# A fused attention and expert layer: the clamped sum in front of a tile's last row maximum, and GpSimd's work held until it is done

## The chip, the cores and the metric

The kernel runs on 1 core of one Trainium2 chip. The metric is the device time of one execution in microseconds (us); lower is better.

## The reference, cut to what matters

Input x is 4096 tokens of 256 features. The first half of the layer is an attention with 16 heads of 16 features and an additive bias that depends on both tokens:

```
q, k, v      = linear(layernorm(x)), split in 16 heads
scores[h]    = q k^T / 4
logits[i,j,:] = li[i,:] + lj[j,:] + rel_b          (3 relations)
bias[h,i,j]  = sum_r softmax(logits[i,j])[r] * logical_bias[h,r]
scores[h]   += gate[i,h] * bias[h,i,j]
out          = softmax(scores) v, then a linear layer, added to x
```

The second half is a layer norm and a mixture of 8 experts, of which each token takes its best 2; its result is added too.

The softmax over three relations needs two differences of logits per pair of tokens, one exponential each, their sum plus one, and the reciprocal of that.

## The kernel before, in words

There are three stages: `project_inputs`, `attend` and `experts`. The change touches only `attend`.

`attend` goes over 32 query chunks `c` of 128 queries, and in each over 32 key tiles `jt` of 128 keys. Chunks 0 to 23 run in a hardware loop that holds 8 chunks; the others are written out. Each engine has its own instruction queue in an order fixed by hand, and engines wait for each other only by counting semaphores (`s["..."]`).

For one key tile (L879 on, L686 on, L762 on):

- TensorE writes the scores of tile `jt + 1` into `b_sc` (`pe_scores`: first `pe_relation`, L801, for each half, then `pe_products`, L813). Each half has one buffer, so a half is overwritten only when the exponential that read it is done. Then come the first row-maximum pair (`pe_pair`, L832), the value product of tile `jt` (`pe_pv`, L855, which needs both exponentials of `jt`), and the second row-maximum pair.
- ScalarE takes the exponentials of both halves of tile `jt` (L690, 128x1024 each). After an even tile it takes the exponential of two clamped sums (`act_r_exp`, L668). After an odd tile it takes a logarithm and an exponential of the sum that GpSimd made of them (`act_r_inv`, L675 and L677); that is the reciprocal.
- VectorE reduces the two row-maximum pairs, four maxima of 128x512 from a ring of three banks, `b_mx` (`dve_pair`, L716), for the coming query chunks, and then makes one clamped sum (`dve_d`, L708, "the clamp": add a constant per query, take the minimum with 43). After tile 23 it also finishes the maxima of a chunk (`dve_m`, L722 and L726). After the first pair of tile 31 it copies the accumulator (L733).
- GpSimd goes by turns of two tiles, turn `t` being tiles `2t` and `2t + 1`. In a turn it adds the two exponentials (`pool_sum`, L613, "the addition"), in turns 13 and 14 it makes half of `b_cm` for the next chunk (`pool_c`, L604), and then it splits the reciprocal into two f16 parts (`pool_parts`: the cast, L623, and the subtraction, L625).
- SP copies these parts into `b_rst` (L526), from where TensorE reads them as weights for the bias. A unit of 512 keys is four tiles; during one unit SP copies the next, and GpSimd makes the one after that.

The work on the relations runs ahead: turn `t` handles the key group `g = t + 4` (`R_AHEAD`), and the clamp made at tile `jt` has the number `8 + jt + 3` counted from the start of the chunk (`D_AHEAD` is 3). So what turn `t` adds has been clamped some tiles before.

Two buffers hold the clamped sums and two the exponentials, so a clamp also waits until the exponential of two groups before has been taken.

Of the kernel before, what the change touches and what calls it, by code (L numbers as in the profile page):

```python
# [29 lines left out]
NT = S // P  # L30
# [7 lines left out]
UNITS = S // JU  # L38
# [15 lines left out]
PAIRN = PAIRS * MXU  # L54
# [5 lines left out]
R_AHEAD, D_AHEAD = 4, 3  # L60
CLAMP_SLOT, ACC_SLOT = 1, 0
# [5 lines left out]
def step_ring(jt, slot):  # L67

    return START + 4 * jt + 2 * slot + (1 if jt > OUT_AT else 0)


def step_bank(jt, slot):

    return step_ring(jt, slot) % MX_RING
# [23 lines left out]
def identity_into(nc, pool, t, zeroed, made):  # L98

    nc.gpsimd.memset(t, 0.0).then_inc(zeroed, 1)  # L100
    pool.wait_ge(zeroed, 1)
    nc.gpsimd.affine_select(out=t, in_=t, compare_op=ALU.not_equal, fill=1.0, base=0,
                            pattern=[[-1, P]], channel_multiplier=1).then_inc(made, 1)
# [341 lines left out]
def attend(nc, kst, vp, dj_dram, q_dram, c_dram, const_dram, m_dram, att_dram):  # L445

    with ExitStack() as ctx:
# [3 lines left out]
        def sem(name):  # L451
            return ctx.enter_context(nc.semaphore("b_" + name))
# [32 lines left out]
        s = {n: sem(n) for n in names}  # L485
# [111 lines left out]
        def pool_c(pool, x, par, nth, half):  # L597

            if half == 0:
                pool.wait_ge(s[f"cval_in{par}"], 96 * nth)  # L600
                pool.wait_ge(s["m_in"], 32 * (x + 1))
                if not (isinstance(x, int) and x < 2):
                    pool.wait_ge(s["scores_ready"], STEPS * (x - 1))
            nc.gpsimd.tensor_tensor(cm[:, par, half],  # L604
                                    cval[:, par, :, half:H:2].unsqueeze(3).broadcast_to([P, NB, PAIRS, BI]),
                                    eye[:, :].unsqueeze(1).unsqueeze(1).broadcast_to([P, NB, PAIRS, BI]),
                                    ALU.mult).then_inc(s["c_made"], 1)

        def pool_sum(pool, x, g):

            n = 16 * x + g
            pool.wait_ge(s["e_ready"], n + 1)
            nc.gpsimd.tensor_tensor(ex[:, g % 2, 0], ex[:, g % 2, 0], ex[:, g % 2, 1], ALU.add).then_inc(s["sum_ready"], 1)  # L613

        def pool_parts(pool, x, g):

            u, n = g // 2, 16 * x + g
            pool.wait_ge(s["r_ready"], n + 1)
            if not (isinstance(x, int) and x == 0 and u < 2):
                pool.wait_ge(s[f"r_in{u % 2}"], 96 * (UNITS // 2 * x + u // 2))  # L620
            pool.sem_inc(s["pool_waited"], 1)
            slot = 2 * (u % 2) + g % 2
            nc.gpsimd.tensor_copy(rhi[:, slot], ex[:, g % 2, 0]).then_inc(s["hi_ready"], 1)  # L623
            pool.wait_ge(s["hi_ready"], n + 1)
            nc.gpsimd.tensor_tensor(rlo[:, slot], ex[:, g % 2, 0], rhi[:, slot], ALU.subtract).then_inc(s["lo_ready"], 1)  # L625

        @block.gpsimd
        def _(pool):
            identity_into(nc, pool, ident[:, :], s["zeroed"], s["ident_made"])
            nc.gpsimd.memset(cval[:, :, :, :], 0.0).then_inc(s["cval_zeroed"], 1)  # L630
            nc.gpsimd.memset(att[:, :, :], 0.0).then_inc(s["att_zeroed"], 1)
            nc.gpsimd.memset(eye[:, :], 0.0).then_inc(s["eye_made"], 1)
            first_rows = [32 * m + part for m in range(4) for part in range(PARTS) if part < PARTS - 1 or m % 2 == 0]
            for n, row in enumerate(first_rows):
                pool.wait_ge(s["eye_made"], n + 1)
                nc.gpsimd.affine_select(out=eye[:, :], in_=eye[:, :], compare_op=ALU.not_equal, fill=1.0,
                                        base=-row, pattern=[[-PARTS, BI]], channel_multiplier=1).then_inc(s["eye_made"], 1)
            pool.wait_ge(s["eye_made"], len(first_rows) + 1)
            for g in range(R_AHEAD):
                pool_sum(pool, 0, g)  # L640
                pool_parts(pool, 0, g)
            for half in range(2):
                pool_c(pool, 0, 0, 1, half)

            def chunk(c, par, nth, last, slot4):
                for turn in range(2 * UNITS):
                    g = turn + R_AHEAD
                    if g < 2 * UNITS:
                        pool_sum(pool, c, g)
                    elif not last:  # L650
                        pool_sum(pool, c + 1, g - 2 * UNITS)
                    if turn in C_MAPS and not last:
                        pool_c(pool, c + 1, 1 - par, nth + par, C_MAPS.index(turn))
                    if g < 2 * UNITS:
                        pool_parts(pool, c, g)
                    elif not last:
                        pool_parts(pool, c + 1, g - 2 * UNITS)

            in_chunks(pool, chunk)


# [39 lines left out]
        def dve_d(dve, x, par, nth, g, n):  # L701

            u, side = g // 2, g % 2
            if g == 0 and n == 0:
                dve.wait_ge(s[f"const_in{par}"], 80 * nth)
            if n == 0 and not (isinstance(x, int) and x == 0 and g < 2):
                dve.wait_ge(s["e_ready"], 16 * x + g - 1)
            nc.vector.tensor_scalar(dl[:, side, n], dj[:, u, n], const[:, par, side, n:n + 1], EXP_MAX, ALU.add,  # L708
                                    ALU.min).then_inc(s["d_ready"], 1)

        def dve_pair(dve, x, n, bank):

            for ab in range(2):
                dve.wait_ge(s["mx_ready"], 2 * PAIRN * x + 2 * n + ab + 1)
                head, part = 2 * (n // MXU) + ab, n % MXU
                nc.vector.tensor_reduce(mxp[:, head, part:part + 1], mx[:, (bank + ab) % MX_RING, :], AX.X,  # L716
                                        ALU.max).then_inc(s["mx_used"], 1)
# [11 lines left out]
        def dve_acc(dve, c):  # L729

            dve.wait_ge(s["pv_done"], NT * c + NT)
            dve.wait_ge(s["o_turned"], c + 1)
            nc.vector.tensor_copy(oT[:, :, :], acc[:, :, :]).then_inc(s["acc_read"], 1)  # L733
# [11 lines left out]
        @block.vector  # L745
        def _(dve):
            nc.vector.memset(oT[:, :, :], 1.0).then_inc(s["acc_read"], 1)
            nc.vector.memset(rst[:, :, :, :], 1.0).then_inc(s["ones_made"], 1)
            dve.wait_ge(s["dj_in0"], 32)
            for n in range(PAIRN):  # L750
                if n % 2 == 0 and n < 2 * R_AHEAD:
                    for k in range(2):
                        dve_d(dve, 0, 0, 1, n // 2, k)
                dve_pair(dve, 0, n, 2 * n)
            dve_m(dve, 0, 0, 1)
            for n in range(AHEAD):
                dve_pair(dve, 1, n, 2 * PAIRN + 2 * n)
            dve.wait_ge(s["dj_in1"], 16 * (UNITS - 2))
            for n in range(D_AHEAD):
                dve_d(dve, 0, 0, 1, R_AHEAD + n // 2, n % 2)  # L760

            def chunk(c, par, nth, last, slot4):  # L762
                more = not last and not (isinstance(c, int) and c + 2 >= NT)
                for jt in range(NT):
                    for slot in range(2):
                        n = 2 * jt + slot + AHEAD
                        if n < PAIRN and not last:
                            dve_pair(dve, c + 1, n, step_bank(jt, slot))
                        elif n >= PAIRN and more:
                            dve_pair(dve, c + 2, n - PAIRN, step_bank(jt, slot))  # L770
                        if slot == CLAMP_SLOT:
                            g, k = R_AHEAD + (jt + D_AHEAD) // 2, (jt + D_AHEAD) % 2
                            if g < 2 * UNITS:
                                dve_d(dve, c, par, nth, g, k)
                            elif not last:
                                dve_d(dve, c + 1, 1 - par, nth + par, g - 2 * UNITS, k)
                        if n + 1 == PAIRN and not last:
                            dve_m(dve, c + 1, 1 - par, nth + par)
                        if jt == NT - 1 and slot == ACC_SLOT:
                            dve_acc(dve, c)  # L780
                    if jt == OUT_AT:
                        dve_out(dve, c)

            in_chunks(dve, chunk)
            dve_out(dve, NT)

# [682 lines left out]
```

## Time and profile before

| | before |
|---|---|
| time, median of 3 runs | 4546.25 us (4544.65 to 4565.15) |
| profiled execution: time | 4540.25 us |
| profiled execution: span | 4538.5 us |
| granted TensorE clock, mean of the span | 0.944 |
| VectorE (DVE) busy | 3815.9 us, 84% |
| TensorE (PE) busy | 3592.7 us, 79% |
| ScalarE (ACT) busy | 3321.6 us, 73% |
| GpSimd (POOL) busy | 2042.4 us, 45% |

The attention loop takes the stretch from about 343 to 3680 us; before it are the projections and the row maxima of the first chunks, and behind it are the experts. The shares are means over all three stages. Times in the rows are us, "mean ns" is of one instruction.

### The profile page before, as it was taken

What the parts mean: (1) busy time and instruction counts of PE and PEld (TensorE: products, weight loads), DVE (VectorE), ACT (ScalarE), POOL (GpSimd) and SP (SyncE); (2) the same over time, 40 slices, a digit from 0 to 9 for tenths busy, and PEclk for the clock granted to TensorE, in tenths of its full rate; (3) what the DMA queues carried; (4) which work ended last, traced back from release to release, by engine and by line L of the source; (5) the groups of instructions that cost most, each with busy time, mean ns of one, the idle gap of its engine ahead of it and who ended that gap; (6) DMA issues with size and microseconds to landing.
All of it is one profiled execution on the core that took longest, in us unless ns stands there. A gap on an engine that the chain in (4) does not pass through costs nothing. (4 is left out here: it accounts for less than half of the span.)

```text
span 4538.5 us, 243862 instructions
## 1 busy us (share of the span) xinstructions
PE 3592.7 (79%) x106896; PEld 2680.9 (59%) x106896; DVE 3815.9 (84%) x6310; ACT 3321.6 (73%) x3946; POOL 2042.4 (45%) x1816
## 2 busy tenths in 40 slices
PE   7548888888888888888888888888888866399991
PEld 4306666666566666656666666666666655277771
DVE  4299999999899999999999999999999814277773
ACT  2008888988898898988898989999999961144440
POOL 0014445554454555544454555555555531533335
PEclk8659999999999999999999999999999996699996
DMA  5312222222222222222222222222222244344433
GB/s 105 73 38 68 67 68 68 71 70 66 65 70 67 67 69 70 66 67 68 66 70 67 71 69 68 68 70 66 75 64 70 67 120 140 121 151 147 154 127 120
DMA packets 368338, 371.66 MB, mean 82 GB/s; under 512 B 108416, under 2 KB 342272, under 8 KB 363296
## 3 DMA queue, kind: packets, MB, share of 16 engines
q1 hardware_dynamic: 358080, 338.08, 27.3%
q8 instruction: 857, 14.04, 1.3%
q0 software_dynamic: 6144, 16.79, 1.2%
q14 instruction: 217, 1.78, 0.1%
q10 hardware_dynamic: 3040, 0.98, 0.1%
HBM read 99.58 MB, written 46.40 MB: 32 GB/s over the span
## 5 line engine op out<-in xcount | busy, mean ns | idle before, releaser
L716 DVE TENSOR_REDUCE b_mxp<-b_mx 128x1 f32<-128x512 f32 x4096 | 2572.8, 679 | 126.5 <-PE b_mx L832 102.2
L690 ACT ACTIVATE b_pr<-b_sc 128x1024 f32<-128x1024 f32 x2048 | 1982.0, 1020 | 418.5 <-PE b_sc L813 399.8
L855 PE MATMUL b_acc<-b_pr,vp 128*32 128x128 f32 x32768 | 1141.4, 276 | 29.5 <-issue 27.1
L832 PE MATMUL b_mx<-kst,b_qt 64*128 64x512 f16 x4096 | 818.9, 393 | 413.1 <-DVE b_mxp L716 397.1
L855 PEld LDWEIGHTS b_acc<-b_pr,vp 128*32 128x32 f32 x32768 | 845.6, 110 | 287.4 <-issue 281.7
L613 POOL TENSOR_TENSOR b_ex<-b_ex 128x512 f32<-128x512 f32 x512 | 679.3, 1327 | 604.8 <-ACT b_ex L668 599.4
L801 PE MATMUL b_sc<-b_cm,b_rst 64*128 64x64 f16 x32768 | 765.8, 191 | 169.4 <-ACT b_pr L690 90.4
L801 PEld LDWEIGHTS b_sc<-b_cm,b_rst 64*128 64x128 f16 x32768 | 657.6, 95 | 338.1 <-ACT b_pr L690 147.0
L708 DVE TENSOR_SCALAR b_dl<-b_dj,b_const 128x512 f32<-128x512 f32 x1024 | 774.1, 758 | 67.9 <-ACT b_ex L668 39.2
L623 POOL CAST b_rhi<-b_ex 128x512 f16<-128x512 f32 x512 | 320.5, 626 | 1064.6 <-ACT b_ex L677 761.0
L813 PE MATMUL b_sc<-b_qt,kst 64*128 64x64 f16 x32768 | 686.4, 191 | 45.7 <-issue 42.0
L625 POOL TENSOR_TENSOR b_rlo<-b_ex,b_rhi 128x512 f16<-128x512 f32 x512 | 633.9, 1238 | 41.0
L813 PEld LDWEIGHTS b_sc<-b_qt,kst 64*128 64x128 f16 x32768 | 571.7, 95 | 67.2 <-issue 64.2
L832 PEld LDWEIGHTS b_mx<-kst,b_qt 64*128 64x128 f16 x4096 | 201.0, 94 | 691.1 <-DVE b_mxp L716 663.8
L668 ACT ACTIVATE b_ex<-b_dl 128x1024 f32<-128x1024 f32 x512 | 541.7, 1058 | 37.4 <-DVE b_dl L708 37.4
L677 ACT ACTIVATE b_ex<-b_ex 128x512 f32<-128x512 f32 x512 | 322.7, 630 | 16.1
L675 ACT ACTIVATE b_ex<-b_ex 128x512 f32<-128x512 f32 x512 | 323.4, 632 | 8.6 <-POOL b_ex L613 8.6
L1314 ACT ACTIVATE c_h<-c_ps,c_b1b 128x512 f32<-128x512 f32 x184 | 126.6, 688 | 276.7 <-PE c_ps L1347 229.7
L1347 PE MATMUL c_ps<-c_xT,c_w1p 128*128 128x512 f16 x1104 | 258.4, 385 | 9.9 <-DVE c_xT L1184 9.8
L1358 PE MATMUL c_ps<-c_w2p,c_a 128*128 128x256 f16 x2208 | 255.4, 273 | 0.0
L1358 PEld LDWEIGHTS c_ps<-c_w2p,c_a 128*128 128x128 f16 x2208 | 216.0, 98 | 36.0
L1071 POOL TENSOR_TENSOR c_w1p<-c_w1r,c_w1p 128x2048 f16<-128x2048 f32 x22 | 90.1, 4094 | 280.2 <-ACT c_w1p L1284 280.2
(144 smaller groups left out, 1753.0 us busy)
## 6 DMA issues: line engine op xcount, KB each, us to landing
b_rst<-b_rhi SPq DMA_DIRECT2D x1024, 128.0 KB
b_rst<-b_rlo SPq DMA_DIRECT2D x512, 128.0 KB
c_w1r<-in_L_ffn_W_dram SPq DMA_DIRECT2D x23, 1024.0 KB, 4.9
c_w2r<-in_L_ffn_W_dram SPq DMA_DIRECT2D x23, 1024.0 KB, 4.9
expert_tokens<-c_zeros SPq DMA_DIRECT2D x23, 512.0 KB, 6.6
c_xb<-expert_tokens SPq DMA_DIRECT2D x23, 512.0 KB
expert_results<-c_y SPq DMA_DIRECT2D x23, 512.0 KB, 2.8
b_qt<-q_parts SPq DMA_DIRECT2D x64, 128.0 KB
```

The lines of the kernel that those rows point to most:

```text
L613: nc.gpsimd.tensor_tensor(ex[:, g % 2, 0], ex[:, g % 2, 0], ex[:, g % 2, 1], ALU.add).then_inc(s["sum_ready"], 1)
L625: nc.gpsimd.tensor_tensor(rlo[:, slot], ex[:, g % 2, 0], rhi[:, slot], ALU.subtract).then_inc(s["lo_ready"], 1)
L668: nc.scalar.activation(ex[:, k].rearrange("p n j -> p (n j)"), dl[:, k].rearrange("p n j -> p (n j)"), ACT.Exp).then_inc(s["e_ready"], 1)
L675: nc.scalar.activation(ex[:, k, 0], ex[:, k, 0], ACT.Ln, bias=1.0).then_inc(s["ln_ready"], 1)
L690: nc.scalar.activation(pr[:, jt % 2, half, :], sc[:, half].rearrange("p a b -> p (a b)"), ACT.Exp).then_inc(s["p_ready"], 1)
L708: nc.vector.tensor_scalar(dl[:, side, n], dj[:, u, n], const[:, par, side, n:n + 1], EXP_MAX, ALU.add, ALU.min).then_inc(s["d_ready"], 1)
L716: nc.vector.tensor_reduce(mxp[:, head, part:part + 1], mx[:, (bank + ab) % MX_RING, :], AX.X, ALU.max).then_inc(s["mx_used"], 1)
L801: ins = pe.matmul(out, rst[rows, u % 2, b, j0:j0 + P], cm[rows, par, half, b], start=(b == 0), stop=False, skip_group_check=True)
L813: ins = pe.matmul(sc[:, ab, side, pair * IS:pair * IS + IS], kst[rows, pair, jt * P:jt * P + P], qt[rows, slot4, pair, side * IS:side * IS ...
L832: pe.matmul(mx[:, (bank + ab) % MX_RING, :], qt[rows, slot4, pair, :], kst[rows, pair, j0:j0 + 512], start=True, stop=True).then_inc(s["mx ...
L855: ins = pe.matmul(acc[32 * (h % 4):32 * (h % 4) + 32, h // 4, :], vp[:, jt, VW * h:VW * h + 32], pr[:, jt % 2, h % 2].rearrange("p (a h i) ...
L1358: ins = pe.matmul(ps[:, 4 + d % 2, 0:D], hT[:, b % 2, hp, f, t * P:t * P + P], w2p[:, b % 2, wp, f, :], start=(f == 0 and hp == 0 and wp = ...
```

## The change

The clamp of a tile stood behind the tile's four row maxima on VectorE; it now stands behind the third and in front of the fourth. GpSimd has two new waits per turn: it goes on to the addition of turn `t` only when VectorE has finished the clamp of tile `2t`, and to the cast only when it has finished the clamp of tile `2t + 1`. `pool_sum` also gets a count on `pool_waited` between that wait and the old one.

```diff
+        def after_clamp(pool, c, jt, last):
+
+            count = 32 * c + 2 * R_AHEAD + D_AHEAD + jt + 1
+            pool.wait_ge(s["d_ready"], min(count, 32 * NT) if last else count)
+
         def pool_sum(pool, x, g):
 
             n = 16 * x + g
+            pool.sem_inc(s["pool_waited"], 1)
             pool.wait_ge(s["e_ready"], n + 1)
...
                 for turn in range(2 * UNITS):
                     g = turn + R_AHEAD
+                    after_clamp(pool, c, 2 * turn, last)
                     if g < 2 * UNITS:
                         pool_sum(pool, c, g)
                     elif not last:
                         pool_sum(pool, c + 1, g - 2 * UNITS)
                     if turn in C_MAPS and not last:
                         pool_c(pool, c + 1, 1 - par, nth + par, C_MAPS.index(turn))
+                    after_clamp(pool, c, 2 * turn + 1, last)
                     if g < 2 * UNITS:
                         pool_parts(pool, c, g)
...
-        def dve_pair(dve, x, n, bank):
-
-            for ab in range(2):
+        def dve_pair(dve, x, n, bank, halves=range(2)):
+
+            for ab in halves:
...
-                        if n < PAIRN and not last:
-                            dve_pair(dve, c + 1, n, step_bank(jt, slot))
-                        elif n >= PAIRN and more:
-                            dve_pair(dve, c + 2, n - PAIRN, step_bank(jt, slot))
-                        if slot == CLAMP_SLOT:
-                            g, k = R_AHEAD + (jt + D_AHEAD) // 2, (jt + D_AHEAD) % 2
-                            if g < 2 * UNITS:
-                                dve_d(dve, c, par, nth, g, k)
-                            elif not last:
-                                dve_d(dve, c + 1, 1 - par, nth + par, g - 2 * UNITS, k)
+                        for ab in range(2):
+                            if slot == CLAMP_SLOT and ab == 1:
+                                g, k = R_AHEAD + (jt + D_AHEAD) // 2, (jt + D_AHEAD) % 2
+                                if g < 2 * UNITS:
+                                    dve_d(dve, c, par, nth, g, k)
+                                elif not last:
+                                    dve_d(dve, c + 1, 1 - par, nth + par, g - 2 * UNITS, k)
+                            if n < PAIRN and not last:
+                                dve_pair(dve, c + 1, n, step_bank(jt, slot), (ab,))
+                            elif n >= PAIRN and more:
+                                dve_pair(dve, c + 2, n - PAIRN, step_bank(jt, slot), (ab,))
```

## Rows read from the trace of the kernel before

**Rows 1.** Busy us (x instructions) by stretch: PE, PEld, DVE, ACT, POOL, clock, DMA.

```profile
343.00:350.00 7.00, 5.58 (x134) 4.05 (x130) 2.74 (x6) 5.97 (x7) 1.26 (x1) 0.50 0.43 115
343.00:3593.00 3250.00, 2719.67 (x98646) 2042.46 (x98640) 3124.68 (x5077) 2924.70 (x3449) 1641.20 (x1537) 1.00 0.26 68
3616.00:3677.00 61.00, 47.08 (x1920) 38.05 (x1911) 20.23 (x22) 58.62 (x70) 30.12 (x31) 1.00 0.27 71
```

**Rows 2.** Waits, 343 to 3593: total us, times, longest us.

```profile
PEld b_mx L832 <- DVE b_mxp L716: 528.4, 933, 1.8
```

**Rows 3.** Instruction groups, 343 to 3593: busy us, mean ns of one, idle before.

```profile
L716 DVE TENSOR_REDUCE b_mxp<-b_mx 128x1 f32<-128x512 f32 x3936 | 2469.8, 679 | 118.8 <-PE b_mx L832 102.2
L708 DVE TENSOR_SCALAR b_dl<-b_dj,b_const 128x512 f32<-128x512 f32 x987 | 740.5, 750 | 0.0
```

**Rows 4.** Timeline of VectorE, 2011 to 2028: start us, duration us, instruction.

```profile
2011.69 1.44 DVE L708 TENSOR_SCALAR b_dl<-b_dj,b_const 128x512 f32<-128x512 f32 x1
2013.05 0.27 DVE L722 TENSOR_REDUCE b_mrow<-b_mxp 128x16 f32<-128x128 f32 x1
...
2022.53 0.71 DVE L708 TENSOR_SCALAR b_dl<-b_dj,b_const 128x512 f32<-128x512 f32 x1
...
2027.71 0.69 DVE L716 TENSOR_REDUCE b_mxp<-b_mx 128x1 f32<-128x512 f32 x1 [0.38 <-PE b_mx L832]
```

**Rows 5.** Timeline of GpSimd, 2011 to 2028.

```profile
2011.57 1.28 POOL L613 TENSOR_TENSOR b_ex<-b_ex 128x512 f32<-128x512 f32 x1 [1.18 <-ACT b_ex L668]
...
2018.66 1.27 POOL L613 TENSOR_TENSOR b_ex<-b_ex 128x512 f32<-128x512 f32 x1 [1.93 <-ACT b_ex L668]
2019.89 1.22 POOL L604 TENSOR_TENSOR b_cm<-b_cval,b_eye 128x512 f16<-128x512 f16 x1
2022.35 0.61 POOL L623 CAST b_rhi<-b_ex 128x512 f16<-128x512 f32 x1 [1.24 <-ACT b_ex L677]
```

**Rows 6.** Timeline of ScalarE, 2015 to 2025.

```profile
2017.53 1.06 ACT L668 ACTIVATE b_ex<-b_dl 128x1024 f32<-128x1024 f32 x1
...
2020.86 0.63 ACT L675 ACTIVATE b_ex<-b_ex 128x512 f32<-128x512 f32 x1
2021.53 0.63 ACT L677 ACTIVATE b_ex<-b_ex 128x512 f32<-128x512 f32 x1
2022.80 1.94 ACT L690 ACTIVATE b_pr<-b_sc 128x1024 f32<-128x1024 f32 x2 [0.64 <-PE b_sc L813]
```

**Rows 7.** Timeline of all engines before the loop, 228 to 231.

```profile
228.93 1.26 POOL L613 TENSOR_TENSOR b_ex<-b_ex 128x512 f32<-128x512 f32 x1 [34.05 <-ACT b_ex L668]
...
230.22 0.63 ACT L675 ACTIVATE b_ex<-b_ex 128x512 f32<-128x512 f32 x1 [1.45 <-POOL b_ex L613]
```

**Rows 8.** Timeline of ScalarE in the last query chunk, 3630 to 3680.

```profile
3630.28 0.63 ACT L675 ACTIVATE b_ex<-b_ex 128x512 f32<-128x512 f32 x1
...
3636.19 0.63 ACT L675 ACTIVATE b_ex<-b_ex 128x512 f32<-128x512 f32 x1
...
3637.39 1.92 ACT L690 ACTIVATE b_pr<-b_sc 128x1024 f32<-128x1024 f32 x2
...
3679.09 0.63 ACT L675 ACTIVATE b_ex<-b_ex 128x512 f32<-128x512 f32 x1
```

**Rows 9.** Timeline of TensorE's matmuls, 2022 to 2028.

```profile
2022.69 0.39 PE L832 MATMUL b_mx<-kst,b_qt 64*128 64x512 f16 x2
2023.01 1.08 PE L855 MATMUL b_acc<-b_pr,vp 128*32 128x128 f32 x32
2024.03 0.39 PE L832 MATMUL b_mx<-kst,b_qt 64*128 64x512 f16 x2
...
2025.51 0.38 PE L832 MATMUL b_mx<-kst,b_qt 64*128 64x512 f16 x2
...
2027.29 0.39 PE L832 MATMUL b_mx<-kst,b_qt 64*128 64x512 f16 x2
```

**Rows 10.** Timeline of TensorE's matmuls at the loop's start, 343 to 350.

```profile
346.54 0.62 PE L832 MATMUL b_mx<-kst,b_qt 64*128 64x512 f16 x2
...
348.96 0.61 PE L832 MATMUL b_mx<-kst,b_qt 64*128 64x512 f16 x2
```

## The prediction, made before the changed kernel was built or run

> **What bounds the kernel now.** I read the busy time by stretch first [rows 1]. The attention stage from 343 to 3593 us is 3250 us long; VectorE is busy for 3125 of them (96%), ScalarE for 2925 (90%), TensorE for 2720 and GpSimd for 1641. In the 61 us of the last query chunk, where no row maxima are left to compute, ScalarE takes over (58.6 us busy) and VectorE falls to 20. So VectorE paces the stage and ScalarE stands right behind it. The waits say the same from the other side: TensorE's weight load for the row-maximum product waited 933 times, 528 us in all, until VectorE had freed a bank [rows 2].
>
> I count in turns: one GpSimd turn spans two key tiles, 2t and 2t+1. The row-maximum work that can tie VectorE to TensorE runs in chunks 0 to 29 (16 turns each) and the first 12 turns of chunk 30, so 492 turns. 3250 us / 492 = 6.61 us per turn now.
>
> In a turn VectorE makes 8 row maxima, 0.68 us each, and 2 clamped sums of mean 0.75 us [rows 3]. A free clamped sum takes 0.47 us, one that meets GpSimd's addition 1.44 us: the addition holds from 2011.57 to 2012.85, the clamp begins at 2011.69 and ends at 2013.13 [rows 4, 5]. That is what the change can win: 987 clamps x (0.75 - 0.47) = 276 us of VectorE's time.
>
> The Trainium skill ("SBUF — State Buffer", section "SBUF: two separate sides") has a rule for this pair of engines: an instruction of the one that uses the shared port pair holds it until it ends, and the other is fully blocked. The 1.44 us clamp agrees. Taken alone, the rule speaks for the change and would have the whole 276 us come back; that result is the third rival below, priced there from rows.
>
> **Where the new wait lands.** This is the step on which everything hangs, so I place the tiles in the trace. The small reduction at 2013.05 is the one that follows key tile 23, so the clamp at 2011.69 is tile 23's, and three clamps on, at 2022.53, is tile 26's [rows 4]. On GpSimd, the product that writes b_cm first comes behind the addition of turn 13; it stands at 2019.89, so the addition at 2018.66 is turn 13's, which belongs to tile 26 [rows 5]. After the change that addition may not start until the clamp of tile 26 is done. Now it starts 3.87 us ahead of that clamp. The ordering is not close: VectorE works on tile 26's maxima long after ScalarE has finished tile 26.
>
> Moving the clamp in front of the last of the tile's four maxima brings it forward by one maximum, 0.61 us. The addition would still be released only at 2022.53 - 0.61 + 0.47 = 2022.39, plus 0.19 us for the signal (an exponential that ends at 2022.16 releases the cast at 2022.35, with the same wait and count in front of it) [rows 5, 6]: 3.92 us later than now. What covers it is small: the addition ends at 2019.93 and ScalarE's logarithm that reads it starts at 2020.86 [rows 5, 6], 0.93 us of cover. And ScalarE runs its queue in order: behind that logarithm wait the second exponential of the same sum and then the two softmax exponentials of tile 28.
>
> **The loop that the wait closes.** Nothing now makes the addition depend on the same tile's clamp; the clamps run three ahead. With the wait there is a ring through all four engines, once per turn. From the end of the clamp of tile 2t:
> - signal to GpSimd 0.19, the addition 1.28, signal to ScalarE 0.03 (an addition that ends at 230.19 releases the logarithm at 230.22) [rows 5, 7]: 1.50;
> - ScalarE: from the logarithm's start to the start of the softmax exponentials of tile 2t+2, 1.20 [rows 8], and those two exponentials, 1.94 [rows 6]: 3.14;
> - TensorE: the scores tensor has one buffer per half, so the scores of tile 2t+3 are finished only after both exponentials of 2t+2, and in the written order they, the first row-maximum pair and the value product all come ahead of the second pair. Exponentials end at 2024.74, pair starts at 2025.51: 0.77. Pair to value product 0.32, value product to the second pair 1.02 [rows 9]: 2.11;
> - from that pair's start to the start of its maximum on an idle VectorE 0.42 (2027.29 to 2027.71) [rows 4, 9], one maximum 0.61, the clamp, alone now, 0.47: 1.50.
>
> Sum 1.50 + 3.14 + 2.11 + 1.50 = 8.25 us per turn. VectorE's own work in it is 8 x 0.61 + 2 x 0.47 = 5.8 us, so it waits; ScalarE's is about the 5.91 us of a turn that it alone paces (3630.28 to 3636.19) [rows 8], so it idles some 2.3 us between the softmax of the odd tile and the late logarithm. Both end below the ring, which therefore is the bound: the collisions on the port are gone and nothing is won by it.
>
> Real turns are a bit longer than clean ones: in the last chunk 8 turns from 3630.28 to 3679.09 take 6.10 us each against 5.91 [rows 8]. Part of such hiccups will fall into engines that now idle; of 0.19 I take 0.15. So 8.40 us per turn, 1.79 more than now, x 492 = 881 us.
>
> **The other parts of the edit.** The cast's wait (for the clamp of tile 2t+1) is in no ring. In the new turn that clamp ends about 2.9 us after tile 2t's does, with the addition (1.28) and, in two turns of sixteen, the b_cm product (1.22) before it on GpSimd, and what the cast feeds, the copies by SP's queue into b_rst, is for a key unit whose use begins four tiles later. I cost it at nothing; the cover is that unit, about two turns. Behind the waiting cast stand the subtraction and the next addition, which waits longer for its own clamp anyway. No DMA is moved; SP's copies only go out later, inside that cover. The additional count on pool_waited rides in the 0.19. The later last maximum (0.47 us) can delay a bank of the ring of three, but the first pair of the next tile needs only the bank of the maximum ahead of the clamp: nothing. In the last chunk, and the last 4 turns of chunk 30, there are no maxima; both clamps of a turn are done before its addition can start, so the waits are met at once and that stretch stays.
>
> Bounds of the ring: what I can't see is whether each piece is as long in the ring as where I read it. With TensorE's and VectorE's pieces read too long by queued work, 8.1 us; with every hiccup on the ring and the 1.22 us product partly on it, 8.9. That is 733 to 1127 us.
>
> The profiled execution took 4540.25 us (span 4538.5), 6 us under the median of 4546.25. 4540 + 881 = 5421, and with those 6 us and the rounding of the ring I say 5430 us. The likeliest case's own range is 5280 to 5680.
>
> **Rivals.**
> - *TensorE's clock drops.* In the ring TensorE idles about 1.9 us in one piece per turn, behind the second pair of the odd tile. The granted clock is 1.00 over the present loop (2.4 GHz) [rows 1]. At 1.2 GHz, as from 343 to 350 us [rows 1], pair to pair takes 2.42 instead of 1.34 us [rows 9, 10]; the 0.77 stretched in that ratio gives 0.62 more, the feeding pair 0.22 more (0.61 against 0.39): the ring is 8.40 + 1.92 = 10.3 us, + 1820 us, some 6370. Against it: at that clock TensorE has almost no idle time in a turn, and after 343 us it was in just such a stretch that it rose. The Trainium skill ("TensorE: Matmul & The Clock Gate", section "Part 1: The HAM clock gate (the 'warmup' mystery)") says that an idle stretch throttles the clock and sustained work releases it; by that this rival would oscillate between both levels and land near 5900.
> - *VectorE keeps its lag.* If the clamp stays as late against ScalarE as now, each turn pays 3.92 - 0.93 = 2.99 us: 9.60 us per turn, +1471, 6020 us. Against it: VectorE has 2.4 us to spare per turn and catches up.
> - *The wait is met in time and the port is what counts.* The other side. If VectorE, relieved, ran so far ahead that the clamp of tile 2t ended before ScalarE's exponential of the same turn, the addition would lose nothing, and the turn would fall by two times 0.28 us, to 6.05; ScalarE's pace of 6.10 [rows 8] is then the bound: (6.61 - 6.10) x 492 = 251 us, so 4295 us. It decides at the point where the lag of 3.9 us is zero; but the maximum in front of that clamp needs a product that TensorE issues behind tile 2t's value product, which needs tile 2t's softmax, and the exponential starts when the softmax ends. The clamp can't come first, since TensorE's 2.11 us and the 1.50 behind it are more than the exponential's 1.06 [rows 6]; this rival needs my reading of the order to be wrong.
> - *A shorter ring.* If TensorE's modelled records overstate its stretch (2.11 becomes 1.3), the ring is 7.5 to 7.6 us: + 460 or so, about 5000 us.
> - *Nothing happens* (the count in the wait is one that is always met): 4546 us. The count is 32c + 12 + tile, and clamps are numbered so that this includes the tile's own.
>
> **Chances.** Forecast 0.76, clock 0.07, lag 0.06, shorter ring 0.05, faster 0.04, nothing 0.02. The range reaches into the shorter ring and the oscillating clock, 5180 to 5760. A difference of under 0.5% (23 us) can't be told from none; slower by more 0.94, within it 0.02, faster 0.04.
>
> **What would show it.** The additions start 8.2 to 8.6 us apart, each about 0.2 us behind the end of a clamp, and the logarithm starts at the addition's end: ScalarE's largest wait becomes GpSimd's addition, about 2 us x 492 = 1000 us in all, where now it is not in the list. Nearly all clamps of the loop take 0.47 us (mean under 0.55). VectorE's busy share of the stretch falls to about 70% and its waits for TensorE's row-maximum product grow by hundreds of us. The third stage keeps its length. I am wrong if the additions keep a spacing under 7.5 us, if ScalarE doesn't wait for GpSimd, or if the granted clock is under 0.95 in the loop.

## The result, and the profile after

| | before | after |
|---|---|---|
| time, median of 4 runs | 4551.01 us (4544.65 to 4565.15) | 5823.51 us (5818.44 to 5830.7) |
| ratio, 95% interval | | 1.2787 (1.2764 to 1.281) |
| profiled execution: time | 4540.25 us | 5819.15 us |
| span | 4538.5 us | 5817.4 us |
| granted TensorE clock, mean | 0.944 | 0.859 |

The change makes the kernel 27.9% slower. I forecast slower, 5430 us with a range of 5180 to 5760; the measured time lies above the range. One execution of the kernel before (5645 us) and one of e12 below (4532 us) ran at a lower granted clock throughout; the ratios leave them out.

Busy time by stretch in the changed kernel, with the columns of [rows 1]. The first row is the loop, the second is the last chunk, the third is the expert stage.

```profile
343.00:4880.00 4537.00, 3222.13 (x98892) 2309.31 (x98896) 2945.73 (x5080) 2948.11 (x3459) 1562.37 (x1541) 0.87 0.19 49
4890.00:4951.00 61.00, 47.89 (x1915) 38.01 (x1906) 19.68 (x24) 58.84 (x71) 30.47 (x31) 1.00 0.27 71
4978.00:5817.00 839.00, 599.90 (x4208) 474.04 (x4208) 470.12 (x825) 253.95 (x312) 331.51 (x189) 0.84 0.42 141
```

All of the loss is in the loop. The last chunk runs as before [rows 1], and in the expert stage, 839 us here, the engines are busy for practically the same time as in the last 838 us of the kernel before (TensorE 600 and 598 us). In the loop VectorE is busy for 65% (96% before) and ScalarE for 65% (90%). No engine bounds it any more. And TensorE's clock is at 0.87 where it was 1.00.

The waits of the loop, 343 to 4880 us, with the columns of [rows 2]:

```profile
POOL b_ex L619 <- DVE b_dl L716: 2165.9, 483, 23.7
DVE b_mxp L724 <- PE b_mx L841: 1562.1, 852, 6.9
...
ACT b_ex L683 <- POOL b_ex L619: 1492.4, 492, 3.8
PE b_sc L810 <- ACT b_pr L698: 1279.6, 1144, 5.0
```

Read as a circle they name the ring: GpSimd waits for the clamp, ScalarE for GpSimd (492 times, the number of turns that the prediction counts), TensorE for ScalarE, VectorE for TensorE. Before, the long wait was TensorE's for VectorE [rows 2], a bounding engine's sign.

Two of the costly groups of the whole changed kernel, with the columns of [rows 3]:

```profile
L724 DVE TENSOR_REDUCE b_mxp<-b_mx 128x1 f32<-128x512 f32 x4096 | 2663.7, 685 | 1586.8 <-PE b_mx L841 1562.1
L716 DVE TENSOR_SCALAR b_dl<-b_dj,b_const 128x512 f32<-128x512 f32 x1024 | 504.5, 494 | 68.0 <-ACT b_ex L676 39.8
```

The clamps fell from a mean of 0.75 us [rows 3] to 0.49 (0.48 in the loop): the collisions are gone. The idle time in front of the maxima, 1587 us, is far more than what that saved.

One turn of the changed kernel, 3006.9 to 3016.7 us, put together from the timelines of the four engines. First GpSimd and ScalarE:

```profile
3006.93 1.27 POOL L619 TENSOR_TENSOR b_ex<-b_ex 128x512 f32<-128x512 f32 x1 [5.12 <-DVE b_dl L716]
...
3016.74 1.27 POOL L619 TENSOR_TENSOR b_ex<-b_ex 128x512 f32<-128x512 f32 x1 [4.63 <-DVE b_dl L716]
```

```profile
3008.24 0.63 ACT L683 ACTIVATE b_ex<-b_ex 128x512 f32<-128x512 f32 x1 [3.21 <-POOL b_ex L619]
...
3009.43 1.92 ACT L698 ACTIVATE b_pr<-b_sc 128x1024 f32<-128x1024 f32 x2
3011.24 1.06 ACT L676 ACTIVATE b_ex<-b_dl 128x1024 f32<-128x1024 f32 x1
```

Then TensorE, and VectorE's maximum and clamp:

```profile
3010.50 0.41 PE L810 MATMUL b_sc<-b_cm,b_rst 64*128 64x64 f16 x16 [2.16 <-ACT b_pr L698]
3011.41 0.41 PE L810 MATMUL b_sc<-b_cm,b_rst 64*128 64x64 f16 x16 [0.51 <-ACT b_pr L698]
3011.65 0.90 PE L822 MATMUL b_sc<-b_qt,kst 64*128 64x64 f16 x32
3012.36 0.62 PE L841 MATMUL b_mx<-kst,b_qt 64*128 64x512 f16 x2
3012.91 1.94 PE L864 MATMUL b_acc<-b_pr,vp 128*32 128x128 f32 x32
3014.77 0.61 PE L841 MATMUL b_mx<-kst,b_qt 64*128 64x512 f16 x2
```

```profile
3015.41 0.69 DVE L724 TENSOR_REDUCE b_mxp<-b_mx 128x1 f32<-128x512 f32 x1 [1.12 <-PE b_mx L841]
3016.02 0.48 DVE L716 TENSOR_SCALAR b_dl<-b_dj,b_const 128x512 f32<-128x512 f32 x1
```

The steps follow each other without a pause. From start to start: the addition to the logarithm 1.31, to the softmax exponentials 1.19, their length 1.92, to the first pair 1.01, to the value product 0.55, to the second pair 1.86, to the clamp 1.25, its length 0.48, the signal 0.24. Sum 9.81 us, the whole turn. The ring is there as predicted; but TensorE's steps are long. The gap of 2.16 us ends at 3010.50, the first products behind it still take 0.41 for sixteen, and then the pair takes 0.62 instead of 0.39 and the value product 1.94 instead of 1.08 [rows 9]. Such durations are those at 1.2 GHz [rows 10], and the granted clock of these stretches, the third number from the end of each row, says the same:

```profile
3005.00:3011.80 6.80, 3.94 (x153) 2.74 (x146) 5.07 (x9) 3.56 (x6) 2.72 (x3) 1.00 0.25 61
3011.90:3015.20 3.30, 3.30 (x66) 2.08 (x60) 1.29 (x2) 2.34 (x3) 0.22 (x1) 0.50 0.40 104
3015.30:3016.70 1.40, 1.40 (x76) 1.17 (x76) 1.29 (x3) 0.00 (x0) 0.00 (x0) 1.00 0.10 29
```

The clock falls behind the gap, when TensorE has begun to work again, and is back before the turn ends.

Between 1000 and 3040 us the trace has 219 steps from one addition to the next: 63 of 8.3 us, 75 of 9.8, most of the rest from 9.2 to 9.7. The mean is 9.29. The 155 steps longer than 8.7 us all hold a stretch with the clock at 1.2 GHz, and the 64 others hold none.

### The profile page after: what moved, and what is told of

It is laid out like the page before. It is cut to its first block and busy times, and to the rows that moved or that the text cites. A ratio compares the mean times of both kernels' runs of the same rounds, so it can differ in the third digit from the quotient of the medians.

```text
span 5817.4 us, 245654 instructions
## 1 busy us (share of the span) xinstructions
PE 4086.5 (70%) x106896; PEld 2939.9 (51%) x106896; DVE 3632.4 (62%) x6310; ACT 3338.7 (57%) x3946; POOL 1959.7 (34%) x1816
## 3 DMA queue, kind: packets, MB, share of 16 engines
q10 hardware_dynamic: 3040, 0.98, 0.1%
## 5 line engine op out<-in xcount | busy, mean ns | idle before, releaser
L724 DVE TENSOR_REDUCE b_mxp<-b_mx 128x1 f32<-128x512 f32 x4096 | 2663.7, 685 | 1586.8 <-PE b_mx L841 1562.1
L810 PE MATMUL b_sc<-b_cm,b_rst 64*128 64x64 f16 x32768 | 855.0, 200 | 1302.4 <-ACT b_pr L698 1294.8
L810 PEld LDWEIGHTS b_sc<-b_cm,b_rst 64*128 64x128 f16 x32768 | 697.9, 101 | 1635.3 <-ACT b_pr L698 1522.2
L864 PE MATMUL b_acc<-b_pr,vp 128*32 128x128 f32 x32768 | 1390.0, 322 | 1.4 <-ACT b_pr L698 1.0
L864 PEld LDWEIGHTS b_acc<-b_pr,vp 128*32 128x32 f32 x32768 | 1026.0, 128 | 319.7 <-issue 287.6
L841 PE MATMUL b_mx<-kst,b_qt 64*128 64x512 f16 x4096 | 922.0, 446 | 132.2 <-DVE b_mxp L724 118.7
L822 PEld LDWEIGHTS b_sc<-b_qt,kst 64*128 64x128 f16 x32768 | 620.8, 100 | 5.0 <-issue 4.6
L631 POOL TENSOR_TENSOR b_rlo<-b_ex,b_rhi 128x512 f16<-128x512 f32 x512 | 592.5, 1157 | 40.9
L716 DVE TENSOR_SCALAR b_dl<-b_dj,b_const 128x512 f32<-128x512 f32 x1024 | 504.5, 494 | 68.0 <-ACT b_ex L676 39.8
L1202 DVE TENSOR_TENSOR c_a<-c_h,c_a 128x512 f16<-128x512 f32 x184 | 210.3, 1143 | 6.3
```

Source lines behind the costliest of these rows:

```text
L810: ins = pe.matmul(out, rst[rows, u % 2, b, j0:j0 + P], cm[rows, par, half, b], start=(b == 0), stop=False, skip_group_check=True)
L822: ins = pe.matmul(sc[:, ab, side, pair * IS:pair * IS + IS], kst[rows, pair, jt * P:jt * P + P], qt[rows, slot4, pair, side * IS:side * IS ...
L841: pe.matmul(mx[:, (bank + ab) % MX_RING, :], qt[rows, slot4, pair, :], kst[rows, pair, j0:j0 + 512], start=True, stop=True).then_inc(s["mx ...
L864: ins = pe.matmul(acc[32 * (h % 4):32 * (h % 4) + 32, h // 4, :], vp[:, jt, VW * h:VW * h + 32], pr[:, jt % 2, h % 2].rearrange("p (a h i) ...
```

## Experiments

Each kernel was timed beside the kernel before on the same chip. "Ratio" is against it, with its 95% interval.

### e1 and e5: keep TensorE at work in the gap

The question was how much of the loss is the ring and how much the clock. Both kernels are the changed one with more work for TensorE: extra products into a bank that the next pair overwrites, in the place where TensorE idles.

The edit, cut to what matters:

```diff
+ # e5, behind every odd tile; e1: tiles 3 to 29 but 23, and FILL = 6
+ pe.wait_ge(s["mx_used"], unit - 1 if jt == OUT_AT else unit - 2)
+ for _ in range(FILL):            # FILL = 8
+     pe.matmul(mx[:, bank, :], qt[0:64, slot4, 0, :], kst[0:64, 0, 0:512], start=True, stop=True)
```

> The changed kernel with added TensorE work: after the second row-maximum pair of each odd tile from 3 to 29, six extra products are issued into the bank that the next tile's first pair will overwrite anyway (about 1.3 us at 2.4 GHz), in the gap in which TensorE idles about 2 us. Nothing of the ring through the four engines changes. Theory (ring of 8.3 us per turn, stretched to 9.2 to 9.8 by the clock that falls in the gap): the granted clock of the loop goes back above 0.95, nearly all turns take 8.3 us, and the time falls to 5430 (5350 to 5550) although TensorE does more. Rival (the ring itself is 9.2 us, the clock is only a sign of the idling): the time stays within 1% of 5824. Rival (VectorE's lag sets it): no less than 5824, rather more.

e1 measured 5640.85 us, ratio 1.2415 (1.2356 to 1.2473). Of 229 turns 133 took 8.3 us, but 65 still took 9.8: only part of the effect, and the forecast was missed. Its trace still shows where the clock falls, behind a gap that was not filled:

```profile
3004.70 0.39 PE L842 MATMUL b_mx<-kst,b_qt 64*128 64x512 f16 x2
3006.60 0.41 PE L811 MATMUL b_sc<-b_cm,b_rst 64*128 64x64 f16 x16 [1.51 <-ACT b_pr L699]
3007.51 0.55 PE L811 MATMUL b_sc<-b_cm,b_rst 64*128 64x64 f16 x16 [0.51 <-ACT b_pr L699]
3007.88 1.04 PE L823 MATMUL b_sc<-b_qt,kst 64*128 64x64 f16 x32
```

> As e1, but eight extra products instead of six, and behind every odd tile (e1 left out tiles 1, 23 and 31, and its full turns still left 0.5 us of the long gap). Clock theory: e1 had 8.3 us turns and 9.8 us turns, the latter where the clock was at 1.2 GHz; with the gap closed the 9.8 us turns nearly vanish, granted clock of the loop above 0.97, mean turn 8.3 to 8.5, time 5400 to 5500. Rival (the long turns come from something else, which the extra products only shift): 5641 as e1 within 1%, or more because of the added work.

e5 measured 5375.69 us (5374.25 to 5375.86), ratio 1.1833 (1.1809 to 1.1856). 235 of 244 turns took 8.3 us. Its loop by stretch, columns of [rows 1], and one turn on TensorE:

```profile
343.00:4430.00 4087.00, 3664.11 (x102612) 2325.55 (x102612) 2959.70 (x5078) 2941.91 (x3451) 1558.54 (x1537) 1.00 0.21 54
```

```profile
3007.08 1.90 PE L868 MATMUL b_mx<-kst,b_qt 64*128 64x512 f16 x8
3008.98 0.41 PE L811 MATMUL b_sc<-b_cm,b_rst 64*128 64x64 f16 x16
3009.89 0.41 PE L811 MATMUL b_sc<-b_cm,b_rst 64*128 64x64 f16 x16 [0.51 <-ACT b_pr L699]
3010.13 0.64 PE L823 MATMUL b_sc<-b_qt,kst 64*128 64x64 f16 x32
3010.61 0.38 PE L842 MATMUL b_mx<-kst,b_qt 64*128 64x512 f16 x2
3010.92 1.08 PE L876 MATMUL b_acc<-b_pr,vp 128*32 128x128 f32 x32
3011.93 0.39 PE L842 MATMUL b_mx<-kst,b_qt 64*128 64x512 f16 x2
```

The eight extra products (1.90 us) fill the gap, the clock stays at 1.00 (2.4 GHz), and the kernel is 448 us faster than the changed one while TensorE does more. The turn now is 8.27 us (additions at 3005.41 and 3013.68), against the 8.25 that was added up beforehand. So of the 1273 us lost, 448 are the clock, and 5376 - 4551 = 825 are the ring at full clock. By the ratios, each taken beside the kernel before on one chip, it is 434 and 834: about a third and two thirds.

### e6 and e7: one wait at a time

```diff
  # e6: the addition's wait alone
  after_clamp(pool, c, 2 * turn, last)
...
- after_clamp(pool, c, 2 * turn + 1, last)
  # e7: the cast's wait alone
- after_clamp(pool, c, 2 * turn, last)
...
  after_clamp(pool, c, 2 * turn + 1, last)
```

> The changed kernel without the cast's wait; the addition still waits for the clamp of tile 2t. Ring theory: the cast is in no ring, so the time is that of the changed kernel, 5824 within 1%. Rival (both waits share the cost): between 4424 and 5824, some 5100.

5828.13 us, ratio 1.2821 (1.2791 to 1.285): all of the loss is the addition's wait.

> The changed kernel without the addition's wait; the cast still waits for the clamp of tile 2t+1. Ring theory: no ring, the time of the moved clamp alone, 4424 within 1%. Rival (both waits share the cost): some 5100.

4564.46 us, ratio 1.0053 (1.0035 to 1.007). A miss: 140 us above the moved clamp alone (e3 below). The cast's wait does close a ring, a longer one that spans two turns. Timelines of GpSimd and ScalarE in this kernel:

```profile
2006.83 0.61 POOL L629 CAST b_rhi<-b_ex 128x512 f16<-128x512 f32 x1 [3.60 <-DVE b_dl L715]
2007.52 1.16 POOL L631 TENSOR_TENSOR b_rlo<-b_ex,b_rhi 128x512 f16<-128x512 f32 x1
2008.64 1.27 POOL L619 TENSOR_TENSOR b_ex<-b_ex 128x512 f32<-128x512 f32 x1
```

```profile
2009.94 0.63 ACT L682 ACTIVATE b_ex<-b_ex 128x512 f32<-128x512 f32 x1 [0.66 <-POOL b_ex L619]
...
2011.14 1.92 ACT L697 ACTIVATE b_pr<-b_sc 128x1024 f32<-128x1024 f32 x2
```

The clamp of the odd tile (ends 2006.58) releases the cast; the subtraction and the next turn's addition are queued behind it with no pause, and ScalarE's logarithm waits for that addition. Clamp to logarithm 3.36, to the softmax 1.20, two tiles of softmax with the exponential between 1.82 + 1.09 + 1.94, TensorE 2.11, to the end of the clamp 1.50: 13.0 us for two turns, 6.5 per turn. The measured mean is 6.70, against 6.42 in e3. The TensorE and clamp pieces of this sum are the prediction's, but the sum shows as a floor: between 1000 and 3000 us none of 296 pairs of turns takes less than 12.9 us, where in e3 202 of 310 do. Clamps that meet GpSimd's instructions (mean 0.56 us, against 0.50 in e3) are not in it. In the changed kernel this ring hides behind the longer ring.

### e4 and e8: make the ring longer and shorter

e4 is the changed kernel with the clamp back behind the fourth maximum; e8 has it in front of the third.

```diff
- if slot == CLAMP_SLOT and ab == 1:
+ if slot == CLAMP_SLOT and ab == 0:      # e8
```

> Only the two waits of GpSimd; the clamp stays behind the fourth maximum. Ring theory: the ring gains one maximum, 0.61 us, so 8.3 + 0.6 = 8.9 us at full clock, and with the same stretches at 1.2 GHz some 9.8 to 10.0 on average: 5824 + 492 x 0.61 = 6120 us (6050 to 6250). Rival (VectorE is not in the path, its order is free): 5824 within 1%.

6337.43 us, ratio 1.3958 (1.3894 to 1.4022). The direction is right and the size isn't: 514 us more than the changed kernel, not 300, and above the range. Nearly every turn takes 10.2 us (185 of 198), and the granted clock of the loop is 0.83: with the longer gap the clock falls in every turn, 194 times in 194 turns between 1000 and 3000 us, against 152 times in 215 in the changed kernel. Per turn e4 costs 1.04 us more, of which the maximum is 0.61; what is left goes with the clock.

> The changed kernel with the clamp in front of the third of the tile's four maxima instead of the fourth; both waits stay. The ring then doesn't pass the value product (1.02), the step from the first pair to it (0.32) and takes one maximum more on VectorE behind the first pair (0.61): 8.3 - 1.34 + 0.61 = 7.5 to 7.6 us at full clock, 0.75 less than the changed kernel. With the clock held, (7.55 - 6.6) x 492 + 4545 = 5010 us; with it falling as often as now some 5450. So 5000 to 5450. Rival (the order on VectorE doesn't matter, the wait costs its 3 us against ScalarE anyway): 5800 within 2%. Rival (only VectorE's maximum ahead of the clamp counts, as between the changed kernel and the waits-only one): 5824 - 0.61 x 492 = 5520.

5025.03 us, ratio 1.1062 (1.104 to 1.1085). 216 of 268 turns take 7.5 us, where 7.5 to 7.6 had been added up; the clock of the loop is 0.95. One turn, from the addition at 2003.50 to that at 2011.03, put together from TensorE, VectorE and GpSimd:

```profile
2008.69 0.38 PE L841 MATMUL b_mx<-kst,b_qt 64*128 64x512 f16 x2
2009.00 1.08 PE L864 MATMUL b_acc<-b_pr,vp 128*32 128x128 f32 x32
2009.11 1.29 DVE L724 TENSOR_REDUCE b_mxp<-b_mx 128x1 f32<-128x512 f32 x2 [1.75 <-PE b_mx L841]
2010.31 0.47 DVE L716 TENSOR_SCALAR b_dl<-b_dj,b_const 128x512 f32<-128x512 f32 x1
2011.03 1.27 POOL L619 TENSOR_TENSOR b_ex<-b_ex 128x512 f32<-128x512 f32 x1 [2.83 <-DVE b_dl L716]
```

The clamp comes 1.62 us behind the start of the first pair, and the value product runs beside the two maxima in between: the ring no longer passes it. The rival by which only one maximum counts would give 8.27 - 0.61 = 7.66 us at full clock; 7.53 was measured. Its price of 5520 us was 500 us off mostly because it left the clock as low as in the changed kernel. Against e5, whose clock stays full, e8 gains 351 us, 0.71 per turn.

### e2: ask for one clamp less

```diff
- count = 32 * c + 2 * R_AHEAD + D_AHEAD + jt + 1
+ count = 32 * c + 2 * R_AHEAD + D_AHEAD + jt
```

> The changed kernel with both new waits asking for one clamp less: the addition of turn t waits for the clamp of tile 2t-1, the cast for that of tile 2t. Theory of the ring: the addition then depends on a clamp whose product was issued before ScalarE's exponential of the same turn, the ring spans two turns with 1.50+1.20+1.94+0.95+1.94+2.11+1.50 = 11.1 us, 5.6 per turn, below ScalarE's 5.9 to 6.1, so it doesn't bind; clamps stay at 0.48 us. ScalarE bounds: 6.1 to 6.3 us per turn, 4290 to 4400 us, faster than before. Rival (each wait on VectorE costs its signal and the order, whatever clamp it asks for): slower than before by some per cent, 4650 or more. Rival (port gain is nothing on the path): within 1% of before.

4419.37 us, ratio 0.9728 (0.9682 to 0.9774), 20 us above the expected 4290 to 4400 but on the right side: faster than before. Its loop by stretch, and its clamps between 400 and 3400 us:

```profile
343.00:3460.00 3117.00, 2743.41 (x98222) 2031.14 (x98222) 2897.36 (x5055) 2896.48 (x3435) 1552.73 (x1531) 1.00 0.27 71
```

```profile
L716 DVE TENSOR_SCALAR b_dl<-b_dj,b_const 128x512 f32<-128x512 f32 x943 | 450.2, 477 | 0.0
```

VectorE and ScalarE are both busy for 93%. Between this and the 5824 us of the changed kernel there is one count in each of the two waits.

### e3, e9 to e12: what the moved clamp is worth

e3 and e12 are the same kernel: the clamp in front of the fourth maximum, no new waits. e9 has it in front of the third, no waits. e10 has it behind the fourth, as before, and both waits as in e2. e11 has it in front of the third and the waits of e2.

> Only the clamp is moved in front of the last row maximum; GpSimd has no new waits (the extra count on pool_waited stays). Ring theory: no ring, so about before: 4550, between 4450 and 4620, since the clamp only meets GpSimd's instructions at other moments. Rival (the move itself costs, by a late bank of the ring of three): 4700 or more. The mean clamp says which: near 0.75 us as before, or shorter if the new place misses the additions.

> The clamp in front of the third maximum, GpSimd without the new waits. The moved clamp alone gave 4424 us, with a mean clamp of 0.50 us instead of 0.75. If the gain of the move is only that clamps miss GpSimd's instructions, it depends on where the clamp then falls: with another 0.6 us earlier it should still mostly miss them, 4400 to 4450, mean clamp under 0.6. Rival (the gain came from the order on VectorE as such, an earlier freed bank): a further gain, 4380 or less, or its loss, 4500 or more, whatever the clamps take.

> The clamp stays behind the fourth maximum as before; GpSimd has both waits, asking for one clamp less than the changed kernel. Ring over two turns: 11.1 + 0.6 = 11.7 us, 5.9 per turn, at ScalarE's own pace, so it may bind a little. All clamps 0.48 us by the waits. If the collisions on the port were the loss of the kernel before, this gets about the same 4420 (4400 to 4480) without the move. Rival (the move's gain is from its place): 4540 within 1%.

> The clamp in front of the third maximum and both waits asking for one clamp less. No ring of one turn; clamps 0.48 us. ScalarE and VectorE both near 5.9 us per turn: 4400 to 4430, the same as e2 within 0.5%. Rival (some 0.6 us of lateness of GpSimd still costs): 20 to 60 us less than e2's 4419.

> The moved clamp alone once more, beside the other candidates on the same chip: 4424 within 0.5%; e2 and it were not told apart.

| | time, us | ratio | mean single clamp, 1000 to 3000 us |
|---|---|---|---|
| before | | 1 | 0.72 |
| e3 | 4423.63 | 0.9737 (0.9691 to 0.9783) | 0.50 |
| e12 | 4454.68 | 0.9775 (0.9754 to 0.9796) | 0.51 |
| e9 | 4441.14 | 0.9748 (0.9726 to 0.9769) | 0.64 |
| e10 | 4462.76 | 0.9795 (0.9775 to 0.9816) | 0.48 |
| e11 | 4451.44 | 0.9766 (0.9739 to 0.9793) | 0.63 |

e3 and e9 to e12 gain 2.0 to 2.6%. e3 was expected between 4450 and 4620 and came out below, a miss: the move alone is worth as much as the move with the harmless waits of e2. e12, its repetition, was expected within 0.5% of 4424 and came out at 4455, in a round in which the kernel before was 15 us slower too; the ratios of e3 and e12 agree.

Without any wait the clamps of e3 and e12 mostly miss the additions. Two forecasts on the clamps missed: in e9 they were expected under 0.6 us and take 0.64, and in e11, expected at 0.48 by its waits, they take 0.63, with a time above the 4400 to 4430 expected. Why the waits of e11 don't keep them apart is open. So the gain does not follow the clamp: e9, with clamps of 0.64 us, is no slower than e12 with 0.51. Between 1000 and 3000 us 235 of its 617 clamps take over 0.55 us, about the share of the kernel before (203 of 604). e10, with no collisions in the old order, gains 2.0%, so the place in the order is not needed for most of the gain; how much of it each of the two causes has in e3 stays open.

The mean turns of these kernels are 6.4 to 6.5 us (6.6 before). ScalarE's own pace, 5.91 us per turn when clean and 6.10 over the last chunk [rows 8], lies under all of these means; what fills the difference was not tested. e2, e3, e9 and e11 can't be told apart; the simplest that beats both kernels is e3, the moved clamp alone.

## Why the prediction was wrong

- **What bounds, and where the wait lands.** Right. In the turn shown the addition starts at 3016.74, 4.4 us after the exponentials that it adds are ready (3012.30), and e6 shows that this wait is the whole loss. The signal from VectorE takes 0.24 us, not the 0.19 of the sum.
- **The ring at full clock, 8.25 us.** Right: 8.27 in e5, 7.5 in e8 where the same pieces less the value product gave 7.5 to 7.6, and 63 turns of 8.3 in the changed kernel itself. It is also what ends the rival in which VectorE keeps its lag (9.60 us per turn).
- **TensorE's piece of the ring.** This is the step that failed. "Pair to value product 0.32, value product to the second pair 1.02", with the 0.77 ahead of them, took 2.11 us from rows at 2.4 GHz. In the turn shown they take 0.55, 1.86 and 1.01, 3.42 us in all, and the step on to the clamp 1.25 instead of 1.03. The sum had TensorE at 2.4 GHz in every turn. The ring makes TensorE idle for 2.2 us once per turn, in 155 turns of 219 the clock falls, and in the turn shown it is low, at 0.50 from 3011.9 to 3015.2 us, just where TensorE's piece lies on the ring. On average that is 448 us / 492 = 0.91 us per turn. The granted clock of the loop, 0.87, is under the 0.95 that the prediction gave as a sign of being wrong.
- **The rival that named this got 0.07.** I argued that at 1.2 GHz TensorE has almost no idle time and so rises again. It does, before the turn is over; and then comes the next gap. A clock that recovers doesn't exclude one that falls again in most turns. Its pair to pair of 2.42 us was right for a slow turn (3012.36 to 3014.77); its 1.39 for the step ahead of it was too long, since the clock fell within that step, which took 1.01. The oscillating price in that paragraph, near 5900, was 1.3% from the measured 5824 and stood beyond the upper end of the range. It was no sum of its own: it is halfway between 5430 and 6370, and how much of a turn the clock would be low was not worked out, so its closeness is luck.
- **Hiccups, 0.15 us per turn.** Too much, without weight: e5's mean turn is 8.34, 0.07 above its clean one.
- **The cast's wait at nothing.** Wrong by itself (140 us, e7), hidden behind the longer ring here (e6 against the changed kernel: 5 us).
- **The clamps.** Right: 0.49 us mean. ScalarE's wait for the addition was forecast at about 1000 us; it is 1492 in the changed kernel and 1107 at full clock, in e5. VectorE's busy share was forecast at about 70% and is 65%.
- **The faster rival.** Its condition, a wait that is met in time, does not hold here. With one clamp less asked for it does: the clamps take 0.48 us and the kernel runs at 0.973. That is still 4419 us and not the 4295 of the rival, and e9 gains as much with collisions about as frequent as before. That the port is the cause of the gain is not shown.

## What to carry to other kernels

Before adding a wait between two engines, follow the awaited instruction back through its operands and through each queue's order: if the path comes back to the waiting one within a turn, the sum of that path is the new period, however idle all engines look. A wait that asks for one item less can leave that ring. And where the new ring leaves TensorE idle once per turn, cost TensorE's steps behind the gap at 1.2 GHz as well, and let the range hold both.

## What the runs showed of the hardware

- With a gap of 2.2 us in TensorE's work per turn the granted clock of the loop was 0.87, where it had been 1.00. Adding useless products in the gap raised it to 1.00 and made the kernel 7.7% faster (5824 to 5376 us).
- Partial filling gave part of it back: e1, which filled 13 gaps of 16 and those not to the end, got 0.92 and 5641 us. e4, with a maximum more on the ring, got 0.83 and was slow in every turn; e8, with the shorter ring, got 0.95.
- A clamp that meets GpSimd's addition takes up to 1.6 us instead of 0.47; the one shown ends 0.3 us after the addition does. The Trainium skill ("SBUF — State Buffer", section "SBUF: two separate sides") calls the shared port pair an exclusive lock; the rows of the kernel before agree (the clamp from 2011.69 to 2013.13 against the addition that ends at 2012.85 [rows 4, 5]). With no such meeting left, in e10, the kernel gained 2.0%.
